# Attention row maxima: turned by a product in the score ring, and moved by SP in one transfer per group

## What is computed

```
xn = layernorm(x)
q, k, v = split(einsum('bsd,hde->bhse', xn, Wqkv) + bqkv)     # 16 heads of 16 channels
score = where(causal, q @ k^T, -inf)
attn  = softmax(score / sqrt(16))                             # maximum, exp, sum
out   = (attn @ v) @ Wout + bout
x     = x + out + ffn(xn)
```

## Time and profile before

| | |
|---|---|
| median of 3 runs | 1206.84 us (1206.24 to 1214.59) |
| span of the profiled execution | 1206.9 us |
| attention stage in it | about 20 to 455 us |
| PE, DVE, ACT, POOL busy, whole span | 92%, 74%, 56%, 44% |
| transfers of the maxima | 128, 1 KB each, on ACT's queue |

### The profile page before, as it was taken

How to read it: one execution, slowest core, us unless ns; L and a number is a source line. 1 busy time by engine, 2 the same in 40 slices (tenths; PEclk the granted TensorE clock), 3 DMA queues, 4 the chain that set the end, 5 groups by cost and what they waited for, 6 DMA issues and landing times. The chain is left out here.

```text
span 1206.9 us, 26712 instructions
## 1 busy us (share of the span) xinstructions
PE 1111.1 (92%) x8873; PEld 745.7 (62%) x8905; DVE 897.4 (74%) x2217; ACT 676.1 (56%) x1463; POOL 529.1 (44%) x743
## 2 busy tenths in 40 slices
PE   4789999999999987998999999996999999999998
PEld 2345555555455546887999888983656646546555
DVE  5778887888888757975766657775876877877876
ACT  2256565555556564565656656664654664664653
POOL 5443434334243235844444444423646547447414
PEclk9689999999999999999999999998999999999999
DMA  5538544354533404665232453452241331331211
GB/s 146 112 67 237 102 80 98 80 111 96 93 81 80 99 19 155 215 179 165 79 127 83 119 163 124 126 149 85 89 141 36 106 126 48 105 102 64 96 45 62
DMA packets 105044, 129.36 MB, mean 107 GB/s; under 512 B 14976, under 2 KB 92736, under 8 KB 103936
## 3 DMA queue, kind: packets, MB, share of 16 engines
q1 hardware_dynamic: 93952, 109.27, 33.8%
q0 software_dynamic: 6912, 18.88, 5.6%
q10 hardware_dynamic: 4096, 0.14, 0.2%
HBM read 84.70 MB, written 43.38 MB: 106 GB/s over the span
## 5 line engine op out<-in xcount | busy, mean ns | idle before, releaser
L537 ACT ACTIVATE p<-bank 128x384 f32<-128x384 f32 (+1 forms) x384 | 191.9, 530 | 186.4 <-PE bank L937 118.8
L757 DVE TENSOR_REDUCE neg_max<-bank 128x1 f16<-128x384 f32 (+3 forms) x352 | 219.7, 640 | 64.7 <-PE bank L925 56.4
L452 POOL TENSOR_SCALAR_AFFINE_SELECT p<-p 128x256 f32<-128x256 f32 x256 | 104.1, 410 | 247.3 <-ACT p L537 246.7
L922 PE MATMUL bank<-k_stack,q_stack 96*128 96x384 f16 (+3 forms) x512 | 133.5, 313 | 20.1 <-DVE neg_max L757 13.1
L1377 POOL DMA_INDIRECT fetched<-xn_dram,token_now x80 | 81.2, 1015 | 42.8 <-POOL token_now L1373 30.6
L937 PE MATMUL bank<-q_stack,k_stack 97*128 97x512 f16 (+1 forms) x256 | 91.5, 362 | 6.0 <-ACT p L537 3.5
L2006 POOL TENSOR_TENSOR up_lo<-up_sq,up_hi 128x512 f16<-128x512 f32 x32 | 43.9, 1399 | 120.7 <-ACT up_hi L2063 120.7
L2017 POOL TENSOR_TENSOR he_lo<-he_sq,he_hi 128x512 f16<-128x512 f32 x64 | 79.9, 1268 | 36.7 <-ACT he_hi L2106 36.6
L1461 ACT ACTIVATE a<-xbank,b 128x256 f32<-128x256 f32 (+1 forms) x126 | 58.6, 468 | 51.2 <-PE xbank L149 47.8
L1549 DVE TENSOR_TENSOR h_lo<-h,h_hi 128x256 f16<-128x256 f32 x159 | 68.4, 433 | 24.4 <-ACT h_hi L1470 23.5
L955 PE MATMUL bank<-p,v_aug 128*32 128x512 f32 (+3 forms) x1024 | 83.5, 445 | 0.8 <-DVE o_rows L737 0.8
(11 more groups left out here) (342 smaller groups left out, 3375.2 us busy)
## 6 DMA issues: line engine op xcount, KB each, us to landing
w_bc<-wT_dram SPq DMA_DIRECT2D x8, 2048.0 KB, 8.0
y_routed_dram<-y SPq DMA_DIRECT2D x37, 256.0 KB
w<-in_w SPq DMA_DIRECT2D x10, 704.0 KB, 6.9
pack<-in_pack SPq DMA_DIRECT2D x12, 342.0 KB, 4.1
xr<-in_x SPq DMA_DIRECT2D x8, 512.0 KB, 7.3
xn_dram<-xn SPq DMA_DIRECT2D x8, 512.0 KB, 3.1
qk_hi_dram<-qk_hi SPq DMA_DIRECT2D x16, 256.0 KB, 2.4
qk_lo_dram<-qk_lo SPq DMA_DIRECT2D x16, 256.0 KB, 2.4
```

Source lines behind the costliest of these rows:

```text
L452: pool.affine_select(out=diagonal, in_=diagonal, pattern=[[0, 2], [1, P]], compare_op=ALU.is_ge, fill=0.0, base=0, channel_multiplier=-1). ...
L537: act.activation(p32[:, s // GH % 2, s % GH, cols], s_bank[n][:, 0:cols.stop - cols.start], ACT.Exp).then_inc(p_exp.sem, 1)
L757: dve.tensor_reduce(neg_max[:, g % 2, 0:GH * TT].rearrange("p (h t) -> p h t", t=TT)[:, heads[0]:heads[-1] + 1, j], a_bank[c % 2][:, 0:len ...
L922: pe.matmul(to[:, at * w:(at + 1) * w], q_stack[0:STK, u, h0 + h, j * P:(j + 1) * P], k_stack[0:STK, u, h0 + h, 0:w], start=at == 0, stop= ...
```

## The change

DVE's block transpose and ACT's four transfers go. In their place PE multiplies neg_max, now f32 and 16 wide, by the identity; the 16 by 128 result goes to the next bank of the score ring, DVE copies it to max_rows (now 16 partitions by 128, f16), and SP sends it in one transfer to row 96 of q_stack. This turn of group g - 1 takes a place of its own in the ring, between units 0 and 1 of group g (TURN_BEFORE = 1), so a group takes 12 places, and units 1 and up change banks. SP's list gets load_max(g) at fixed places, store_hi and store_lo of the second half come before store_xn, and load_shared comes behind the last load_max.

```diff
-AT_MAX = {0: (0, 1), 1: (2, 3)}
+TURN_BEFORE = 1
-        neg_max = sb("neg_max", [P, 2, 32], F16)
-        max_rows = sb("max_rows", [P, 2, 32], F16)
+        neg_max = sb("neg_max", [P, 2, GH * TT])
+        max_rows = sb("max_rows", [GH * TT, 2, P], F16)
-        max_loaded = [sig(f"max_loaded{k}", 16 * 4) for k in range(2)]
+        max_loaded = [sig(f"max_loaded{k}", 16) for k in range(2)]
+        def units_before(g, i):
+            return (AU + 1) * g + i + (1 if i >= TURN_BEFORE else 0)
+        def turned_in(g):
+            return (units_before(g + 1, TURN_BEFORE) - 1) % 2
 # SP
+            def load_max(g):
+                b, h0 = g // NG, GH * (g % NG)
+                sp.wait_ge(max_rows_s.sem, max_rows_s.at(g))
+                to = q_stack[STK:AUG, b % 2, h0:h0 + GH, :].rearrange("o h (t c) -> o (h t) c", t=TT)
+                sp.dma_start(to, max_rows[:, g % 2, :]).then_inc(max_loaded[g % 2].sem, 16)
             store_xn(1)
+            load_max(0)
             for b in range(NB):
                 if b + 2 < NB:
                     load_x(b + 2)
+                load_max(NG * b + 1)
                 if b + 1 < NB:
                     store_xT(b + 1)
                     store_hi(b + 1, 0)
-                if b + 1 < NB:
+                    store_lo(b + 1, 0)
                     load_stacks(b + 1, 0)
+                load_max(NG * b + 2)
+                load_max(NG * b + 3)
                 if b + 1 == NB:
                     sp.wait_ge(xT_stored.sem, xT_stored.at(0))
                     load_shared()
                 if b >= 1:
                     store_x1(b - 1)
+                if b + 1 < NB:
+                    store_hi(b + 1, 1)
+                    store_lo(b + 1, 1)
                 if b + 2 < NB:
                     store_xn(b + 2)
                 if b + 1 < NB:
-                    store_hi(b + 1, 1)
                     load_stacks(b + 1, 1)
+                    load_max(NG * b + 4)
 # ACT
-            def load_max(g, quarters):   # four transfers, one per 32 tokens
...
-                    if at % (U * GH) in AT_MAX and LEAD < group(s) <= GROUPS:
-                        load_max(group(s) - 1, AT_MAX[at % (U * GH)])
 # DVE
-                dve.transpose(max_rows[:, g % 2, :], neg_max[:, g % 2, :]).then_inc(max_rows_s.sem, 1)
+            def copy_turned(g):
+                dve.wait_ge(max_turned.sem, max_turned.at(g))
+                dve.wait_ge(max_loaded[g % 2].sem, max_loaded[g % 2].at(g // 2 - 1))
+                dve.tensor_copy(max_rows[:, g % 2, :], a_bank[turned_in(g)][0:GH * TT, 0:P]).then_inc(max_rows_s.sem, 1)
...
-                        if i < AU:
-                            maxima(group(s), i)
-                        else:
-                            turn_maxima(group(s))
+                    if i == TURN_BEFORE and group(s) <= GROUPS:
+                        copy_turned(group(s) - 1)
+                    if group(s) < GROUPS and i < AU:
+                        maxima(group(s), i)
 # PE, in scores_q
-                if c >= 2:
-                    pe.wait_ge(a_max.sem, c - 1)
+                if i == 0 and g > 0:
+                    pe.wait_ge(a_max.sem, a_max.at(g - 1, AU - 1))
+                elif i == 1:
+                    pe.wait_ge(a_max.sem, a_max.at(g, 1))
+                elif i == 2 and g > 0:
+                    pe.wait_ge(max_rows_s.sem, max_rows_s.at(g - 1))
+                elif i > 2:
+                    pe.wait_ge(a_max.sem, a_max.at(g, i - 1))
 # PE
+            def turn_maxima(g):
+                pe.wait_ge(a_max.sem, a_max.at(g))
+                pe.matmul(a_bank[turned_in(g)][0:GH * TT, 0:P], neg_max[:, g % 2, :], identf[:, :],
+                          start=True, stop=True).then_inc(max_turned.sem, 1)
...
+                    if i == TURN_BEFORE and group(s) <= GROUPS:
+                        turn_maxima(group(s) - 1)
                     if group(s) < GROUPS and i < AU:
                         scores_q(group(s), i)
```

More of the change, by code:

```diff
@@ L235, in mix_phase @@
         tail_filled = sig("tail_filled", 16)
-        cleared = sig("cleared", 2)
+        cleared = sig("cleared", 1)
         x_loaded, wqkv_loaded = carried.x_loaded, carried.wqkv_loaded
@@ L262, in mix_phase @@
         a_max = sig("a_max", AU)
+        max_turned = sig("max_turned", 1)
         max_rows_s = sig("max_rows_s", 1)
-        max_loaded = [sig(f"max_loaded{k}", 16 * 4) for k in range(2)]
+        max_loaded = [sig(f"max_loaded{k}", 16) for k in range(2)]
         s_psum = sig("s_psum", U)
@@ L350, in store_hi, with store_lo @@
                 sp.dma_start(hi_rows, hi_tile).then_inc(qk_stored.sem, 16)
-            def load_stacks(b, half):
-                u, heads = b % 2, slice(half * NH // 2, (half + 1) * NH // 2)
+            def load_max(g):
[3 more added lines that the diff above has]
+                sp.dma_start(to, max_rows[:, g % 2, :]).then_inc(max_loaded[g % 2].sem, 16)
+            def store_lo(b, half):
                 lo_rows = dram["qk_lo"].rearrange("(a m p) s -> p m a s", a=2, p=P)[:, half]
@@ L359, in load_stacks @@
                 sp.dma_start(lo_rows, lo_tile).then_inc(qk_stored.sem, 16)
+            def load_stacks(b, half):
+                u, heads = b % 2, slice(half * NH // 2, (half + 1) * NH // 2)
                 sp.wait_ge(qk_stored.sem, qk_stored.at(2 * b + half))
@@ L385, in _ @@
                 store_hi(0, half)
+                store_lo(0, half)
                 load_stacks(0, half)
@@ L538, in exps @@
                                ACT.Exp).then_inc(p_exp.sem, 1)
-            def load_max(g, quarters):
[L542 to L547, removed]
             def out_copy(g):
@@ L571, in _ @@
             router_exp(0)
-            for g in range(LEAD):
-                load_max(g, range(4))
             for n in range(U):
@@ L611, in _ @@
             dve.memset(run[:, 0, :], 0.0).then_inc(cleared.sem, 1)
-            dve.memset(neg_max[:, :, :], 0.0).then_inc(cleared.sem, 1)
             dve.wait_ge(cleared.sem, cleared.at(0))
@@ L753, in maxima @@
                 heads, j = A_UNITS[i]
-                c = AU * g + i
+                c = units_before(g, i)
                 dve.wait_ge(a_psum.sem, a_psum.at(g, i + 1))
@@ L759, in maxima @@
                                   ALU.max, negate=True).then_inc(a_max.sem, 1)
-            def turn_maxima(g):
-                dve.wait_ge(a_max.sem, a_max.at(g))
+            def copy_turned(g):
+                dve.wait_ge(max_turned.sem, max_turned.at(g))
                 dve.wait_ge(max_loaded[g % 2].sem, max_loaded[g % 2].at(g // 2 - 1))
-                dve.transpose(max_rows[:, g % 2, :], neg_max[:, g % 2, :]).then_inc(max_rows_s.sem, 1)
+                dve.tensor_copy(max_rows[:, g % 2, :], a_bank[turned_in(g)][0:GH * TT, 0:P]).then_inc(max_rows_s.sem, 1)
             def split_shared(n):
@@ L799, in _ @@
                 for i in range(AU):
+                    if i == TURN_BEFORE and g > 0:
+                        copy_turned(g - 1)
                     maxima(g, i)
-                turn_maxima(g)
             for s in range(NB * NH):
@@ L805, in _ @@
                     at, i = U * h + n, U * (s % GH) + n
-                    if group(s) < GROUPS:
-                        if i < AU:
-                            maxima(group(s), i)
-                        else:
-                            turn_maxima(group(s))
+                    if i == TURN_BEFORE and group(s) <= GROUPS:
+                        copy_turned(group(s) - 1)
+                    if group(s) < GROUPS and i < AU:
+                        maxima(group(s), i)
                     for when, part in ((AT_SCORES, router_scores), (AT_CHOICE, router_choice), (AT_RANKS, router_ranks)):
@@ L908, in scores_q @@
             def scores_q(g, i):
-                b, h0, c = g // NG, GH * (g % NG), AU * g + i
+                b, h0, c = g // NG, GH * (g % NG), units_before(g, i)
                 u, to = b % 2, a_bank[c % 2]
@@ L1000, in _ @@
                 for i in range(AU):
+                    if i == TURN_BEFORE and g > 0:
+                        turn_maxima(g - 1)
                     scores_q(g, i)
```

## The result

The changed kernel takes 1253.54 us (median; 1251.05 to 1255.47), the kernel before 1207.61 on the same chip: 1.037 times as long, 95% interval 1.034 to 1.040. The profiled execution has a span of 1253.7 us, 46.8 more than before. All of it arises in the attention stage: the point at which PE turns to slot 0 of the third group of the last batch, 431.76 us before, comes 47.6 us later, and the end of the execution 46.8.

The account below looks back on a forecast made before the run. PE and DVE, handing each other the score ring, were taken to set the pace in turn. Ring 29, queue 12, ACT's relief -6 and last batch 5.6 gave 41 us on 1206.9: 1248 us, range 1205 to 1264.

Parts of the forecast that it names:

- ACT's relief: ACT's sequencer, 2.4 us per group freed of transfer issues: -6 us, ends -13 and 0.
- ring place: Score ring at group boundaries: unit 1 must wait until unit 0 is reduced; 4.15 us a batch, 29 us over 7 batches.
- A: Group boundary followed by SP's stack loads, PE at unit 1 at 217.91: unit 2 comes 0.7 us late.
- B: Group boundary with unit 1 at 230.63: unit 2 comes 2.0 us late, 1.3 us stay after unit 3's wait.
- C: Group boundary with unit 1 at 244.81: unit 1 comes 1.2 us late and all of it stays.
- D: Group boundary with unit 1 at 256.11: PE, not DVE, holds unit 0; unit 1 comes 0.95 us late.
- Product and copy at nothing: PE's product and DVE's copy at boundaries, covered while unit 1 waits: nothing; product uncovered 0.2 to 0.57 us each.
- SP's queue: After A, the maxima land late behind six stack loads: 2.4 us stall, 1.7 us a batch counted, 12 us in all.
- The last batch: load_shared, moved later, stalls ACT 3.2 us; three boundaries at 0.8 us each; together 5.6 us.
- that the queue does not matter: Rival: only the ring costs, the place in SP's queue nothing; 1236 us, chance 0.18.
- rival 2: Absorbed: PE's later waits for DVE shrink as unit 1's grows; a quarter of 29 stays; 1211 us, chance 0.14.
- ACT's sequencer as the bound: Rival: exponentials held behind ACT's four issues end last at boundaries, so the change is faster; 1187 us, chance 0.10.

Follow-up runs that it names:

- spare_sp: Changed kernel with the turned maxima in unit 3's free bank columns, product and copy in slot 3, no ring place, SP's list as changed; 1235.79 us.
- turn_6: Changed kernel with the turn's ring place moved to before unit 6 and the one transfer per group issued by ACT in slot 7; 1263.44 us.
- before_sp_early: Kernel before, old ring and DVE transpose, its four transfers per group moved to SP's new list, maxima after A ahead of the stack loads; 1215.22 us.
- hole: Kernel before with an empty score-ring place between units 0 and 1 of each group, nothing else of the change; 1245.7 us.
- sp_early: Changed kernel with SP's transfer of the maxima after A moved ahead of the six stack loads; 1234.63 us.
- act_queue: Changed kernel with the one transfer per group issued by ACT in slot 2 instead of by SP; 1236.68 us.
- spare_act: Changed kernel with the turned maxima in unit 3's free bank columns, no ring place, one transfer per group issued by ACT in slot 4; 1227.57 us.
- before_sp_late: Kernel before, old ring and DVE transpose, its four transfers per group moved to SP's new list, maxima after A behind the stack loads; 1249.83 us.

## Why the prediction was right, point by point

The forecast was 1248 us, 1205 to 1264, and the measured 1253.5 lies 5.5 above it. The cause is the one named, shown by taking each part away and by making each alone. That the number is so near is in part luck: the term for SP's list was 8.7 us too small and that for the ring with ACT's relief 3, against 3.2 us at the end that were not lost.

*The ring place*: right. Forecast 29 us, less 6 for ACT, plus 2.4 for the last batch: 25.4. Measured in slots 0 to 7: 35.3 - 7.1 = 28.2. By boundary, slots 0 to 2 are longer by 0.8 at A (forecast 0.7), 2.3 at B (1.3, after 0.69 taken back; measured net of slots 3 to 7 it is 2.1), 1.0 at C (1.2) and 0.7 at D (0.95). B was mis-sized most: I let unit 3's wait swallow 0.7 us, and slot 3 gave back 0.3 on average.

*Product and copy at nothing*: right where they stand, since PE idles 0.6 to 1.5 us between product and unit 1. Their price without that cover was sized between 0.2 and 0.57 us, and slot 3 of spare_sp shows 0.35, slot 6 of turn_6 0.42. The copy took 269 ns and not 214; it does not matter, because DVE still idles 0.41 us behind it.

*ACT's relief*: the size fits, but no run isolates it in the changed kernel. Forecast -6; with the old ring, before_sp_early shows -6.3 us in slots 3 to 7 and -2.3 in the lead-in. The -7.1 of the changed kernel in slots 3 to 7 cannot be booked to it, since hole has -6.5 there with all of ACT's issues. The 42.2 us of idle time marked "issue" that ACT had ahead of its exponentials are gone from the changed kernel's list, as forecast.

*SP's queue*: the mechanism, a transfer that lands late behind the six loads and holds PE, was right, the size too small. Forecast 1.7 us a batch, 12 in all; measured 20.7 by sp_early. The stall itself was forecast at 2.4. Slot 8 is longer by 2.2 to 3.1 us in six of the batches, 2.5 on average, and by 4.5 in the first, partly at half the clock; the last landing I had put at 6 us after the issue, and it was 6.3. What failed is the deduction of 0.7 us a batch for small waits behind it. In the four batches with the full clock there slot 9 is shorter by 0.33 us, and slots 10 and 11 are as before. In the other three slots 9 to 11 are at half the clock for 1.7 to 1.9 us, which I had not seen coming, and 0.5 to 0.8 us longer. Over the seven batches slots 9 to 11 cost 0.5 us, where I had deducted 4.9. I had given two reasons why it was no cost before, that ACT issued the maxima on a queue of its own, and sooner. Only the second shows in the runs (act_queue, spare_act, turn_6).

*The last batch*: wrong in load_shared. I gave it the landing time of 7.5 us that it had behind the stack loads. At its new place no stack loads stand ahead of it, and ACT is not held up:

```profile
482.65 0.38 SPq L343 DMA_DIRECT2D xn<-in_w  x1
...
DMA to landing us min/median/max: 3.5/3.5/3.5
...
486.19 0.79 ACT L575 ACTIVATE shared_in<-xr 128x704 f16<-128x704 f32 x1
```

The second load was issued at 482.65 and landed 3.5 us later, at 486.15; ACT went on to its first reader at 486.19, with no idle time on record. The 3.2 us were not lost. The same rule that made the maxima late makes this load early, and I had applied it to one and not to the other.

*The rivals*: that the queue does not matter (1236) describes sp_early, at 1234.6, and not the change. Absorption was small: later slots gave back 7.1 us of 35.3, and 6.5 of 39.5 in hole, where rival 2 wanted three quarters. ACT's sequencer as the bound does not fit before_sp_early: it takes all issues from ACT and was to be under 1190, and even without the 14 us that its two waits for transfers grew by it would be at 1201.

Section Queues, rings and completion order of "DMA: Bandwidth & Descriptors" in the Trainium skill gives SP and ACT a ring each on the same DMA engines, each ring consumed in order. The runs agree as far as a transfer behind the loads on SP's queue lands after them (6.3 us). That each engine takes turns between the rings would let one expect that ACT's small transfer gets by; it did not here, with 6.4 us in act_queue, 5.5 in spare_act and 4.9 in turn_6, and the measurement decides. The sentence in Key Constraints of "Trainium Kernel Development and Optimization" in the Trainium skill, that issuing from several engines only saves issue time, fits these landings. That the queue is then no cost, as the prediction worked it out, is not what was measured: the order of SP's list alone makes 1253.5 or 1234.6 us.

## What to carry to other kernels

Count a ring's free places at the moment at which its consumer is furthest behind, not on average: the same place cost 37 us at a boundary and nothing five units later. Issue a small transfer that others wait for before the bulk loads. Another engine's queue helps only if it lets the transfer be issued sooner: issued on ACT's queue beside the stack loads of A and C it took 4.4 to 7.8 us in spare_act, and mostly 1.6 to 1.8 without such loads. Moving it also moves the loads behind it, which may be just in time themselves. Two such delays in one cycle hide part of each other, so measure each alone before summing.

## What the runs showed that I had not expected

PE's granted clock falls behind some of the waits, and that can make the slots behind them longer as well. In the changed kernel, after PE's idle stretch of 2.88 us up to 251.5 (columns as above, clock third from the end):

```profile
252.00:257.00 5.00, 4.88 (x28) 2.90 (x26) 3.43 (x11) 2.87 (x6) 1.02 (x3) 0.66 0.00 0
...
257.00:262.00 5.00, 4.12 (x33) 3.13 (x34) 3.35 (x10) 1.18 (x3) 1.82 (x3) 1.00 0.02 4
```

In 252 to 257 the granted clock is 0.66 on average: for 3.4 us it is at half, 1.2 GHz, and then at 2.4 again. The kernel before has 1.00 from 74 to 442 us. Such stretches come in four of the seven batches of the changed kernel, and in its first one of 10.2 us, where the kernel before has 6.8; the mean clock of the whole execution is 0.971, from 0.980. It is not the transfer's wait alone that they follow: hole, which waits only for the ring, has three of them, and sp_early one. In before_sp_late, where the stalls are longest, the mean clock is 0.964, and slots 9 to 11 after A, which have no wait for the transfer, are 9.2 us longer. By batch the two go together: in three batches these slots are at half the clock for 4.5 us and 1.8 us longer, in the one with the least, 1.8 us at half, they are 0.5 us longer. In sp_early the mean clock is back at 0.978 and they are as before. In the changed kernel this cost is small: PE's seven waits sum to 22.4 us, and sp_early is 20.7 faster.
